# A first feed-forward stage rebuilt in three token groups, and two steps of the state stage moved ahead, on one core

## The reference, cut to what matters

```python
def _L0_ffn_ref(x, w1, conv_w, conv_b, w2):
    h = bit_linear(x, w1)                 # 256 -> 1024
    h = depthwise_conv1d(h.transpose(0, 2, 1), conv_w, conv_b)   # 3 taps along the 37 tokens
    h = h.transpose(0, 2, 1)
    h = jax.nn.silu(h)
    return bit_linear(h, w2)              # 1024 -> 256
# act_quant: scale = 127 / max|x| of a token; round(x * scale), clipped, / scale
# weight_quant: scale = 1 / mean|w| of the matrix; round(w * scale) clipped to -1..1, / scale
h = h + _L0_ffn_ref(_layernorm(h, axis=-1), ...)
```

## Time and profile before

| | |
|---|---|
| median of 3 runs (lowest, highest) | 1965.34 us (1962.55, 1969.71) |
| the profiled execution: own time, span | 1968.07 us, 1966.2 us |
| PE busy / weight loads | 1463.4 us (74%) / 1150.1 us |
| DVE busy | 1421.6 us (72%) |
| ACT busy | 809.7 us (41%) |
| POOL busy | 605.7 us (31%) |

### The profile page before, as it was taken

One profiled execution on the slowest core, in us unless ns is written; L12 is line 12 of the kernel. 1 busy time (PEld: TensorE's weight loads), 2 busy tenths in 40 slices (PEclk: granted clock), 3 DMA queues, 4 the chain that ended last, 5 costly groups with the idle time before them and its releaser, 6 DMA issues. The chain is left out here.

```text
span 1966.2 us, 23839 instructions
## 1 busy us (share of the span) xinstructions
PE 1463.4 (74%) x8427; PEld 1150.1 (58%) x8427; DVE 1421.6 (72%) x2307; ACT 809.7 (41%) x1553; POOL 605.7 (31%) x410
## 2 busy tenths in 40 slices
PE   3897323479999946867768962887768889779797
PEld 3575102369998423434457952775357789567697
DVE  7586677898665589999755744787976477675666
ACT  5475220365553755555213531762233243333332
POOL 1500002122220039999506315236122141100320
PEclk9997555889999978898968986899889989878899
DMA  3511000111100211240047612002443010320110
GB/s 97 108 29 44 1 0 0 52 50 43 44 1 29 84 67 60 77 128 9 2 156 170 168 59 51 25 14 43 131 99 87 22 46 9 77 32 1 42 33 26
DMA packets 65313, 108.76 MB, mean 55 GB/s; under 512 B 34750, under 2 KB 43549, under 8 KB 63583
## 3 DMA queue, kind: packets, MB, share of 16 engines
q1 hardware_dynamic: 57218, 92.96, 16.1%
q0 software_dynamic: 6416, 9.29, 2.5%
q10 hardware_dynamic: 1562, 5.00, 0.8%
HBM read 83.82 MB, written 18.13 MB: 52 GB/s over the span
## 5 line engine op out<-in xcount | busy, mean ns | idle before, releaser
L2535 POOL TENSOR_TENSOR c_dbub<-c_dub,s_bcb 128x814 f32<-128x814 f32 x96 | 169.8, 1793 | 85.4 <-DVE c_dub L2604 72.6
L2580 PE MATMUL c_pc<-c_st,ident 128*128 128x407 f32 x384 | 158.9, 562 | 49.1 <-POOL c_st L2543 42.7
L2519 ACT ACTIVATE c_da<-s_deltab,s_ab 128x407 f32<-128x407 f32 x192 | 108.1, 595 | 119.1 <-DVE c_st L2630 101.4
L2580 PEld LDWEIGHTS c_pc<-c_st,ident 128*128 128x128 f32 x384 | 77.6, 210 | 127.8 <-POOL c_st L2543 58.6
L2626 DVE TENSOR_TENSOR_SCAN c_da<-c_da,c_dbub 128x814 f32<-128x814 f32 x60 | 110.6, 1843 | 0.0
L3315 DVE SCALAR_TENSOR_TENSOR dc_acc<-dc_pp,dc_cw,dc_acc 128x1311 f32<-128x1311 f32 x48 | 75.8, 1584 | 21.7 <-ACT dc_acc L3232 20.2
L2045 ACT ACTIVATE e_sg<-e_pu,e_b 128x444 f32<-128x444 f32 (+1 forms) x96 | 56.7, 591 | 80.2 <-PE e_pu L1971 74.7
L2126 DVE TENSOR_TENSOR e_sg<-e_sg,e_gate 128x444 f32<-128x444 f32 (+1 forms) x96 | 54.6, 570 | 48.1 <-ACT e_sg L2045 45.1
L1933 POOL TENSOR_TENSOR e_wlb<-e_wb,e_whb 128x1024 fp32r<-128x1024 f32 x16 | 42.2, 2659 | 126.0 <-ACT e_whb L2020 126.0
L2814 POOL DMA_INDIRECT me_xe<-m_xs,mt_rowsb x48 | 48.4, 1008 | 77.6 <-DVE mt_rowsb L2980 37.0
L2543 POOL TENSOR_TENSOR c_st<-c_st,s_bcb 128x814 f32<-128x814 f32 x36 | 68.9, 1914 | 4.8 <-DVE c_st L2623 4.8
(11 more groups left out here) (698 smaller groups left out, 4619.6 us busy)
## 6 DMA issues: line engine op xcount, KB each, us to landing
s_bcb<-s_bc SPq DMA_DIRECT2D x48, 407.0 KB, 3.9
m_wb<-in_m_w SPq DMA_DIRECT2D x16, 768.0 KB, 7.8
e_wb<-in_e_w SPq DMA_DIRECT2D x4, 2048.0 KB, 7.5
m_ys<-me_yb SPq DMA_DIRECT2D x16, 384.0 KB
d_z<-d_first ACTq DMA_DIRECT2D x11, 384.0 KB, 2.7
d_first<-d_z SPq DMA_DIRECT2D x11, 384.0 KB, 3.5
le_wb<-in_l_w_e SPq DMA_DIRECT2D x9, 384.0 KB, 3.1
de_wb<-in_d_w_e SPq DMA_DIRECT2D x8, 384.0 KB, 3.0
```

The lines of the kernel that those rows point to most:

```text
L2519: last = nc.scalar.activation(da[k % 2][:, c * CH:(c + 1) * CH], delta[:, t, c0 + c, :], ACT.Exp, scale=a[:, n, c0 + c:c0 + c + 1])
L2535: nc.gpsimd.tensor_tensor(wide(dbu[k % DB][:, :]), du[:, t, c0:c0 + HC, :], bc[n][:, 0:1, :].broadcast_to([P, HC, CH]), ALU.mult).then_inc ...
L2580: last = nc.tensor.matmul(pc[:, c, 0:CH], ident[:, :], st[k % YB][:, c * CH:(c + 1) * CH], start=False, stop=(n == N - 1), skip_group_chec ...
```

## The change

`stage_ffn0` is written anew as one block.

- The layer norm runs in the same block as the rest. The tokens' largest magnitudes are taken by halves; rounding and clipping goes over a half at a time (`rounded`). ACT scales w1 and w2 (`Copy` with a scale); DVE rounds and clips them (`ternary`), w2 only after unit 3 of the loop.
- The token factor is multiplied into the input instead of into the product: ACT multiplies the rounded tiles by it (`weighed`), PE turns them in float32, ACT writes the fp32r part `xh` (`high`) and DVE the rest `xl`. Both are laid out with zeros between sequences (`SP` = 40 columns for 37 tokens), so that the taps can run over the product in PSUM. w1 is fp32r. A product has four matmuls (two halves of the contraction, `xl` and `xh`).
- The loop has 24 units, group by chunk: 480, 480 and 360 columns wide. Four PSUM banks `f_pp` and four tiles `f_acc` rotate. For a unit ACT applies the first tap, DVE taps 1 and 2 straight from PSUM, ACT silu and a new `Abs` into `f_ab` (`magnitude`), DVE one maximum (`largest`, two units late). ACT's order is silu(i), magnitude(i), first tap(i+2).
- After chunk 3 of a group, DVE takes the scales of the group before (`scales`); in chunks 4 to 7 it scales, rounds and clips one pair of chunks of the group before (`scaled`, `whole`, `clipped`), and in the last group also adds four projected tiles. The remaining work (scales of the last group, seven adds and three tiles of rounding) follows the loop. POOL has no part in it any more.

In `stage_scan` the four diagonals and the product `du` for `t` = 0 move from the loop block to the opening block, `du` shares memory with `e`, and the products for `t` = 1 and 2 are made after steps 6 and 12.

```diff
         @block.tensor
+            def project(i):
+                g, c = UNITS[i]
+                lo, hi = GROUPS[g]
+                if c == 0:
+                    pe.wait_ge(s["xl"], KC * (g + 1))
...
+                if i >= PB:
+                    pe.wait_ge(s["taps"], i - PB + 1)
+                dst = pp[i % PB][:, 0:width(g)]
+                for k in range(KC):
+                    w = w1q[:, k, c * P:(c + 1) * P]
+                    nc.tensor.matmul(dst, w, flat2(xl[:, k, lo * G:hi * G, :]), start=(k == 0), stop=False)
+                    last = nc.tensor.matmul(dst, w, flat2(xh[:, k, lo * G:hi * G, :]), start=False, stop=(k == KC - 1))
+                last.then_inc(s["mm"], 1)
...
+            for i, (g, c) in enumerate(UNITS):
+                project(i)
+                if g and c == 5:
+                    turn_maxima(g - 1)
+                if g and c == 6:
+                    spread(g - 1)
+                if g == NS - 1 and 4 <= c < 4 + 4:
+                    project_out(c - 4)
+            turn_maxima(NS - 1)
+            for n in range(4, 8):
+                project_out(n)
+                if n == 5:
+                    spread(NS - 1)
+            for n in range(8, NT):
+                project_out(n)
         @block.scalar
+            act.wait_ge(s["half"], 1)
+            weighed(*HALVES[0])
+            high(0)
+            act.wait_ge(s["half"], 2)
+            weighed(*HALVES[1])
+            high(1)
+            high(2)
+            first_tap(0)
+            first_tap(1)
+            for i in range(NU):
+                silu(i)
+                magnitude(i)
+                if i + 2 < NU:
+                    first_tap(i + 2)
+                if i == 0:
+                    nc.scalar.activation(w2[:, :], w2[:, :], ACT.Copy, scale=wscale[:, 1:2]).then_inc(s["w2s"], 1)
         @block.vector
+            def scaled(m):
+                one, _ = part(m)
+                g = min(m // (FC // PIECE), NS - 1)
+                at = max(m - FIRST, 0) * TT
+                dve.wait_ge(s["bc_mm"], g + 1)
+                dve.wait_ge(s["ab"], FC * (g + 1))
+                nc.vector.tensor_tensor(one, one, pb[:, at:at + one.shape[2]].unsqueeze(1).broadcast_to(list(one.shape)),
+                                        ALU.mult).then_inc(s["scaled"], 1)
...
+            for i, (g, c) in enumerate(UNITS):
+                m = (g - 1) * FC // PIECE + c - 4 if g and c >= 4 else None
+                tap(i, 1)
+                if m is not None:
+                    scaled(m)
+                elif i >= 2:
+                    largest(i - 2)
+                tap(i, 2)
+                if m is not None:
+                    whole(m)
+                    largest(i - 2)
+                    clipped(m)
+                if i == 3:
+                    dve.wait_ge(s["w2s"], 1)
+                    ternary(w2, w2q, "w2q")
+                if g and c == 3:
+                    scales(g - 1)
+                if g == NS - 1 and c >= 4:
+                    add(c - 4)
```

```diff
@@ stage_scan, opening block, DVE
                 nc.vector.tensor_scalar(a[:, :, :], a[:, :, :], -1.0, None, ALU.mult)
+                dve.wait_ge(sg["in"], 96)
+                for c in range(C):
+                    nc.vector.tensor_scalar(dg[:, c, :], ident[:, :], dd[:, c:c + 1], None, ALU.mult)
...
-                    nc.vector.scalar_tensor_tensor(df, df, 0.0, e[:, t, :], ALU.max, ALU.add)
+                    ins = nc.vector.scalar_tensor_tensor(df, df, 0.0, e[:, t, :], ALU.max, ALU.add)
+                    if t == 0:
+                        dve.wait_ge(sg["xc"], C)
+                        link(ins)
+                        nc.vector.tensor_tensor(du[:, t, :, :], delta[:, t, :, :], xc[:, t, :, :], ALU.mult)
@@ loop block, DVE
-                nc.vector.tensor_tensor(du[:, 0, :, :], delta[:, 0, :, :], xc[:, 0, :, :], ALU.mult
-                                        ).then_inc(s["c_du"], 1)
-                for c in range(C):
-                    nc.vector.tensor_scalar(dg[:, c, :], ident[:, :], dd[:, c:c + 1], None, ALU.mult
-                                            ).then_inc(s["c_dg"], 1)
-                moved_in(1)
...
-                    if k == 6:
-                        moved_in(2)
+                    if k in (6, 12):
+                        moved_in(k // 6)
```

More of the change, by code:

```diff
@@ L885, in stage_ffn0 @@
     FC = F // P
-    SP = S + 2
+    SP = S + 3
+    NS = len(GROUPS)
+    UNITS = [(g, c) for g in range(NS) for c in range(FC)]
+    NU = len(UNITS)
+    PB, RING, AB = 4, 4, 4
+    PIECE = 2
+    FIRST = (NS - 1) * FC // PIECE
     with ExitStack() as stack:
         sb, ps = bufs(nc, stack)
+        s = fresh(nc, stack, " ".join(f"f_{x}" for x in (
+            NORM_SEMS + " w1_in w2_in c_in ones wsum wtot scales w1s w2s w1q w2q half xq edge xh xl mm tap0 taps silu "
+            "ab amax mx_turned mx diag bc_mm tap1 scaled whole hq out_mm out").split()))
+        s = {k[2:]: v for k, v in s.items()}
         x = sb("f_x", [TT, NT, D])
@@ new lines, in silu, with magnitude @@
+            def silu(i):
+                g, c = UNITS[i]
+                act.wait_ge(s["taps"], i + 1)
+                own = acc[i % RING][:, 0:width(g)].rearrange("p (b j) -> p b j", j=SP)[:, :, 0:S]
+                nc.scalar.activation(act1[:, c, tokens(g)].rearrange("p (b j) -> p b j", j=S), own, ACT.Silu
+                                     ).then_inc(s["silu"], 1)
+            def magnitude(i):
+                g, c = UNITS[i]
+                act.wait_ge(s["silu"], i + 1)
+                a, b = GROUPS[g]
+                if c == 0:
+                    dst = amax[:, tokens(g)]
+                else:
+                    if i >= AB and maxima(i - AB):
+                        act.wait_ge(s["amax"], maxima(i - AB))
+                    dst = ab[i % AB][:, 0:(b - a) * TT]
+                nc.scalar.activation(dst, act1[:, c, tokens(g)], ACT.Abs).then_inc(s["ab"], 1)
@@ new lines, in whole, with clipped, add @@
+            def whole(m):
+                one, _ = part(m)
+                dve.wait_ge(s["scaled"], m + 1)
+                nc.vector.tensor_scalar(one, one, ROUND, -ROUND, ALU.add, ALU.add).then_inc(s["whole"], 1)
+            def clipped(m):
+                one, dst = part(m)
+                dve.wait_ge(s["whole"], m + 1)
+                nc.vector.tensor_scalar(dst, one, 127.0, -128.0, ALU.min, ALU.max).then_inc(s["hq"], 1)
+            def add(n):
+                dve.wait_ge(s["out_mm"], n + 1)
+                nc.vector.scalar_tensor_tensor(h[:, n, :], po[n % 2][0:TT, 0:D], hinv[:, n:n + 1], h[:, n, :], ALU.mult,
+                                               ALU.add).then_inc(s["out"], 1)
@@ L1140, in layout_ffn0 @@
+            for i in range(NU - 2, NU):
+                largest(i)
+            scales(NS - 1)
+            for n in range(4, 8):
+                add(n)
+            last = range(FIRST, FIRST + NT - GROUPS[-1][0])
+            for m in last:
+                scaled(m)
+            for m in last:
+                whole(m)
+                if m > FIRST:
+                    clipped(m - 1)
+            clipped(last[-1])
+            for n in range(GROUPS[-1][0], NT):
+                add(n)
 def layout_ffn0(i, o):
```

397 lines of the change are left out of this document (189 added, 208 removed).

## The result

The changed kernel takes **1915.43 us** (median of 4 runs, 1910.12 to 1919.82), the kernel before 1964.82 beside it: ratio **0.9744**, 95% interval 0.9712 to 0.9776. Forecast were 1912 and 1900 to 1928. The profiled execution has its own time of 1919.82 and a span of 1917.6 us, against a span of 1966.2 before.

What follows compares the result with a forecast made beforehand. DVE was taken as the bound, in the feed-forward stage and in the state loop with POOL close behind. 1968.07 - 49.2 - 4.4 = 1914.5 us for an execution like the profiled one, 2.7 above its median: 1912, range 1900 to 1928.

Steps and rivals of the forecast that it cites:

- barriers, entry and exit: Feed-forward stage's edges: one barrier goes, the other costs 1.29 instead of 2.38 us; 1.1 us gained.
- before the loop: Feed-forward stage up to the end of the first tap: norm, maxima, rounding, weights and input tiles; 27.4 us.
- loop: Feed-forward chunk loop, three token groups of 19.4, 26.1 and 25.0 us: 70.5 us, against 76.8 before.
- tail: Feed-forward work after the loop: 15.0 us, or 20.6 with PE at the lower clock; 16.5 taken, against 45.9 before.
- state stage: First scan 7.4 us sooner, one more `c_dub` in the loop at 3.0: -4.4 us in sum.
- The unit: Plain loop unit: DVE 1.80 and ACT 1.75 us, nearly level and coupled, so 1.89 each; 1.58 for 360 columns.
- PE stays at the lower clock: Rival, chance 0.13: feed-forward loop unchanged, tail +4.1 us, spreads late by some tenths; 1917 us.
- If the tail waits on PE: Sign that the prediction is wrong: the feed-forward work after the loop waits for PE; no size given.
- Hand-offs show: Rival, chance 0.13: each of the ring's five steps costs 0.2 us more, about 0.6 per plain unit; +10, 1922 us.
- looser coupling: Rival, chance 0.07: DVE at 1.80 us per loop unit and no stalls for the spread; -4, 1908 us.
- slower: Rival, chance 0.02: fp32r products cost as much as float32 ones, feed-forward loop 153 us; +83, 1995 us.
- the rival in its own form: Rival, chance 0.10: POOL bounds the state loop and wins only its own earlier start, 1.5 us; +3, 1915 us.

Runs made afterwards that it cites:

- abs_back: Changed kernel with `Abs` taken off ACT and the maxima made by two DVE instructions again; ratio to the kernel before 0.9767, stage 129.2 us.
- lead2: Changed kernel with PE allowed at most two units ahead of the taps instead of four; ratio to the kernel before 0.9743, stage 121.7 us.
- warm_tail: Changed kernel with 24 products that nothing reads before the last turn of the maxima; ratio to the kernel before 0.9711, stage 117.9 us.
- f32_products: Changed kernel with two float32 products per unit instead of four fp32r ones, and no `xl`; ratio to the kernel before 0.9732, stage 119.6 us.
- scan_fill: Changed kernel with `du` for the second third of the tokens made at the state loop's opening again; ratio to the kernel before 0.9742, state loop 249.7 us.
- tail_order: Changed kernel with the last spread one product earlier on PE and `scaled` dealt between the last adds; ratio to the kernel before 0.9705, stage 115.4 us.
- no_clip: Changed kernel without clips to -128 and 127 on values just scaled to their own maximum; ratio to the kernel before 0.9692, stage 111.6 us.
- undealt: Changed kernel with scaling, rounding and clipping of all three token groups behind the loop; ratio to the kernel before 0.9751, stage 126.3 us.

## Why the prediction was right

| step | forecast | measured |
|---|---|---|
| barriers, entry and exit | -1.1 | -0.2 |
| before the loop | 27.4 | 27.37 |
| loop | 70.5 | 69.8 |
| tail | 16.5 | 17.7 |
| stage | -49.2 | -47.8 |
| state stage | -4.4 | -3.7 |

*Barriers.* Mis-sized: I took 1.29 us twice; they are 1.69 and 1.76, with 2.38 and 1.29 before.

*Before the loop.* The total is right in part by luck, as two errors cancel. DVE was done with rounding 0.8 us sooner than I had it (21.6 us in, not 22.4), and ACT's four `high` took 0.4 less. But the first tap then waited 1.25 us for PE's first products, which I had put at nothing ("lie beside these"):

```profile
217.41 0.75 ACT L1049 ACTIVATE f_acc<-f_pp,f_cb,f_cw 128x478 f32<-128x478 f32 x1 [1.25 <-PE f_pp L971]
```

The operation that no row showed, a float32 pass with fp32r output, took 1.23 us (L1225), so of the bounds 0 and 1.0 it is 0.

*The unit.* Right: 1.88 for 1.89. `abs_back` shows the two halves of the argument apart, DVE's own 1.8 and 0.1 of coupling. Chunks 4 to 7 took 3.83 and 3.85 (3.88 and 3.92 forecast). By groups the loop took 19.7, 25.2 and 24.9 us against 19.4, 26.1 and 25.0. Here too errors cancel. The start-up costs more, since I had left out Silu's table load (1.28) from the path, and in group 3 DVE waits 0.63 for the turned maxima, where I had counted nothing. The dealt chunks cost less, and the spread stalls are 0.21 and 0.34 instead of 0.75 each: PE's spread took 1.01 us, where I had 1.6 at the lower clock.

*The clock.* Here the rival "PE stays at the lower clock" was half right. The granted clock goes to and fro between its levels, in loop and tail. In the loop that costs next to nothing, because of the lead of four units (`lead2`: 3 us without it). The tail is 17.7 us, 2.7 over my sum for the higher clock, of which I had allowed 1.5. Two places meet the lower level: the turn and the first projections, for 1.8 us by `warm_tail`, and a part of the last burst, which took 4.14 us where the rate of the earlier trace rows gives 2.8. My own guess was that PE would be at the high level as it works right up to the tail. It idled 7.7 us before the turn, and the granted clock is 0.50 and 0.55 behind that. The rule that I cited from the Trainium skill ("TensorE: Matmul & The Clock Gate", section "Why this matters for your kernels"), that idle gaps between bursts take the clock back, fits that better. "If the tail waits on PE" was one of my signs of being wrong, and it came: DVE waits 5.2 of the 17.7 us for PE.

*Hand-offs show, looser coupling, slower:* none of them. The units hold 1.88, and products that cost twice as much per unit (two of 0.84 us for four of 0.22) still fit (`f32_products`).

*State stage.* The shift of the first scan was right (7.9 against the block's opening; the block itself opens 358.0 us behind the feed-forward stage, 357.9 before, so the 0.45 that I gave the barrier doesn't show). One term was mis-sized and one missing: the additional `s_dub` costs 1.8, not 3.0 (2.74 + 1.84 in the loop, 2.77 before), and DVE now waits 1.47 and 1.71 us for out-projections at two adds to `h` where it had waited 0.37 and nothing. -7.9 + 1.8 + 2.8 = -3.3 of the 3.5 by which the loop shortened. POOL never made a scan wait, so the rival in its own form fell. Why the out-projections are late is **open**: in `scan_fill` the first of the two waits is 0.37 and the second stays (1.60), in `tail_order` and `warm_tail` the second is missing with the same code. POOL's work, the clock and PE's order all touch them, and no run separates these.

The median is 3.4 us over the forecast. The profiled execution, which has a trace, is 5.0 over by its span (1917.6 against 1966.2 - 49.2 - 4.4 = 1912.6): 2.1 from the two stages above (1.4 and 0.7), 2.3 ahead of the feed-forward stage and 0.6 behind the state stage, where nothing was changed. The last two are inside the spread of single runs.

What stays argued: no run takes the rewrite of the feed-forward stage apart by its pieces ahead of the loop, the move of the token factor from the product to the input, or POOL's part in the scaling. Their shares come from rows alone. Shown by runs are the price of DVE's instructions (`abs_back`, `no_clip`), the waits that dealing closes (`undealt`) and PE's lead (`lead2`).

## What to carry to other kernels

Where one engine is nearly always busy, price its instructions one by one and count the waits apart. `no_clip` came out by the first. `undealt` needed the second, and there I had it wrong: dealing work into a loop paid by waits closed and not by work hidden. Before calling a wait "start-up", name the instruction that fills it: here a table load and a weight scaling, both of which had idle time ahead of the loop. And an instruction moved into a gap must be priced beside what the other engine does in that gap: the 2.7 us taken out of the state loop came back as 3.3 us of contention.
